# Moving half of the output projection, its addition and its statistics into the last attention pair of a macaron transformer kernel

## The reference, cut to what matters

```python
x = x + 0.5 * ffn(layernorm(x))       # 32 experts, top 8, capacity 128
x = x + attention(layernorm(x))       # 16 heads, causal, ends in "attn @ W_o"
x = x + 0.5 * ffn(layernorm(x))       # the same experts again

def ffn(h):
    logits = h @ gate_weight.T
    topw, topi = top_k(softmax(logits), 8)
    # tokens take their place in each expert's buffer in order (cumulative count of the
    # choices), go through gate/up/silu/down, and are added back by their weight
```

## Time and profile before

| what | us |
|---|---|
| median of 3 runs | 598.95 |
| the 3 runs | 602.34, 598.62, 598.95 |
| the profiled execution | 601.41 |
| its span | 599.4 |

### The profile page before, as it was taken

One profiled execution on the slowest core, in us unless ns is written; L12 is line 12 of the kernel. 1 busy time (PEld: TensorE's weight loads), 2 busy tenths in 40 slices (PEclk: granted clock), 3 DMA queues, 4 the chain that ended last, 5 costly groups with the idle time before them and its releaser, 6 DMA issues.

```text
span 599.4 us, 11028 instructions
## 1 busy us (share of the span) xinstructions
PE 539.6 (90%) x3522; PEld 338.8 (57%) x3546; DVE 425.6 (71%) x1423; ACT 260.3 (43%) x430; POOL 89.8 (15%) x208
## 2 busy tenths in 40 slices
PE   6979999878798999999999999999988876899995
PEld 2856778653454555555555555555533653577774
DVE  5786989764776776767687676767800697689873
ACT  2643212234554555465555546554576241121212
POOL 2320000011601122121212112121222050000000
PEclk8789999987998999999999999999999898899998
DMA  9775100000161000000000000000000440000002
GB/s 190 142 226 177 43 1 3 1 2 2 44 238 55 2 26 29 28 25 11 23 26 26 29 28 25 12 20 28 0 2 1 126 112 1 1 3 2 1 3 70
DMA packets 25094, 26.70 MB, mean 45 GB/s; under 512 B 6704, under 2 KB 18576, under 8 KB 25040
## 3 DMA queue, kind: packets, MB, share of 16 engines
q1 hardware_dynamic: 24176, 25.63, 15.1%
q10 hardware_dynamic: 864, 0.36, 0.2%
HBM read 17.04 MB, written 8.78 MB: 43 GB/s over the span
## 4 chain that ended last, share of the span: by engine, by line
PE 69%; DVE 18%; issue 5%; ACT 4%; DMA 2%; SPq 1%; DVEq 0%; POOL 0%; ACTq 0%
PE ps L1520 12%; PE ps L1585 11%; PE ps L1236 10%; PE ps L1558 9%; PE ps L1320 6%; PE ps L1335 4%; DVE mxh L1078 3%; PE ps L1350 2%; DVE summed L1075 2%; PE ps L1516 2%; DVE xn L802 2%; PE ps L1227 2%; ACT probs L717 2%; PE ps L1162 1%; DMA x<-in_L_attn_x 1%
## 5 line engine op out<-in xcount | busy, mean ns | idle before, releaser
L717 ACT ACTIVATE probs<-ps 128x1024 f32<-128x1024 f32 (+2 forms) x192 | 148.2, 810 | 116.5 <-PE ps L1558 116.4
L1078 DVE TENSOR_REDUCE mxh<-ps 128x1 f32<-128x512 f32 (+2 forms) x176 | 117.4, 690 | 46.3 <-PE ps L1520 44.5
L1520 PE MATMUL ps<-Kst,Qst 120*128 120x512 f32 (+3 forms) x384 | 132.1, 410 | 7.1 <-DVE mxh L1078 3.9
L1520 PEld LDWEIGHTS ps<-Kst,Qst 120*128 120x128 f32 x384 | 66.5, 191 | 64.5 <-DVE mxh L1075 23.3
L1558 PE MATMUL ps<-Qst,Kst 121*128 121x512 f32 (+3 forms) x384 | 95.6, 355 | 1.9 <-ACT probs L717 1.7
L1075 DVE CUSTOM_DVE_ANT_0 summed<-ps,maskf 128x384 f32<-128x384 f32 (+1 forms) x128 | 76.0, 620 | 22.3 <-PE ps L1520 20.3
L490 POOL TENSOR_SCALAR_AFFINE_SELECT probs<-probs 128x256 f32<-128x256 f32 x128 | 52.0, 406 | 220.9 <-ACT probs L717 220.2
L1585 PE MATMUL ps<-probs,Vst 128*32 128x512 f32 (+3 forms) x768 | 81.8, 498 | 1.2 <-POOL probs L490 1.2
L1558 PEld LDWEIGHTS ps<-Qst,Kst 121*128 121x128 f32 x384 | 67.0, 190 | 22.5 <-ACT probs L717 7.3
L1236 PE MATMUL ps<-onehot,xp 128*128 128x512 bf16 (+1 forms) x251 | 68.8, 399 | 9.9 <-DVE onehot L878 8.5
L878 DVE TENSOR_SCALAR onehot<-iotab,posm 128x128 bf16<-128x128 bf16 (+1 forms) x352 | 60.1, 248 | 0.1
(11 more groups left out here) (179 smaller groups left out, 625.1 us busy)
## 6 DMA issues: line engine op xcount, KB each, us to landing
wgn<-in_L_ffn_gate_up_proj SPq DMA_DIRECT2D x8, 384.0 KB, 5.6
guT_d<-gus SPq DMA_DIRECT2D x6, 384.0 KB, 2.8
gus<-guT_d SPq DMA_DIRECT2D x6, 384.0 KB, 6.0
Kst<-kn_d SPq DMA_DIRECT2D x28, 64.0 KB
Qst<-qn_d SPq DMA_DIRECT2D x28, 64.0 KB
wdn<-in_L_ffn_down_proj SPq DMA_DIRECT2D x8, 192.0 KB, 5.9
dnT_d<-dns SPq DMA_DIRECT2D x6, 192.0 KB, 3.9
dns<-dnT_d SPq DMA_DIRECT2D x6, 192.0 KB, 6.9
```

The source lines that it names most:

```text
L717: e.activation(probs[n % RING][:, 2 * b:2 * b + 2, lo:BANK], ps[:, 2 * b:2 * b + 2, lo:BANK], ACT.Exp, scale=SCALE).then_inc(probs_ready, 1)
L1078: e.tensor_reduce(to, s.rearrange("p (q k) -> p q k", k=w), AX.X, ALU.max).then_inc(mx_ready, 1)
L1520: ins = e.matmul(ps[:, bank, i * w:(i + 1) * w], Qst[p][h][0:ROWS, column(b, jt * P):column(b, jt * P) + P], Kst[p][h][0:ROWS, column(b, o ...
```

## The change

For tokens 0 to 511 of both sequences (now called groups 0 and 2, first in the new order HORDER), the last pair of heads is finished by step 8. The change moves these two groups' turning, product with W_o, copy, addition and statistics into the last pair: PE turns them in step 9 and multiplies them in step 10, DVE does the copies, the additions, statistics, mean and variance (`half_early`) ahead of the last `normalise`. After the pair only groups 1 and 3 are left for PE, and DVE begins with the normalised rows of groups 0 and 2; the additions and statistics of groups 1 and 3 come after these, ahead of the first choice of experts (`choose_second`). The stages after attention take the groups in the order 0, 2, 1, 3. The square root's table is loaded ahead of the last copy of attention. The idle products change: 6 and 2 new ones around the last `turn_out`, 2 instead of 20 ahead of the first turned group of rows, and others as shown.

```diff
+HORDER = (0, 2, 1, 3)
+ORDER = ((0, 1, 2, 3), YORDER, HORDER)
+TORDER = ((0, 1, 2, 3), YORDER, HORDER, HORDER)
+WBANK = (6, 7, 2, 3)
...
 (ScalarE)
             pair_step(NPAIR - 1, 1, 0)
+            table_for(ACT.Sqrt)
             copy_values(NPAIR - 1, 1)
-            table_for(ACT.Sqrt)
-            transposed(2)
             root(2, 0)
             root(2, 1)
+            turned_out(2, 2)
+            turned_out(2, 3)
+            first_part(1, 0)
+            first_part(1, 1)
             turned_out(3, 0)
-            root(2, 2)
-            first_part(1, 0)
-            root(2, 3)
             turned_out(3, 1)
             copy_logits(1, 0)
+            root(2, 2)
+            root(2, 3)
             table_for(ACT.Exp)
-            first_part(1, 1)
+            copy_logits(1, 1)
             turned_out(3, 2)
-            copy_logits(1, 1)
             first_part(1, 2)
...
 (VectorE)
+            def half_early():
+                for i in range(RING):
+                    e.wait_ge(turned, 2 * NG + i + 1)
+                    e.tensor_copy(xnT[:, HORDER[i] * BANK:(HORDER[i] + 1) * BANK], ps[:, turn_bank(2, i), :]).then_inc(xnT_ready, 1)
+                for i in range(RING):
+                    add(1, i)
+                for i in range(RING):
+                    stat(2, i)
+                for i in range(RING):
+                    moment(2, i)
+                    variance(2, i)
+                normalise(NPAIR - 1, 1)
+                norm(2, 0)
+
+            def choose_second():
+                norm(2, 1)
+                rest_of(1, 0)
+                add(1, 2)
+                stat(2, 2)
+                add(1, 3)
+                stat(2, 3)
+                moment(2, 2)
+                variance(2, 2)
+                moment(2, 3)
+                variance(2, 3)
+                rest_of(1, 1)
+                norm(2, 2)
+                best(1, 0)
+                norm(2, 3)
+                choice(1, 0)
+                best(1, 1)
+                choice(1, 1)
+                rest_of(1, 2)
+                best(1, 2)
+                choice(1, 2)
+                best(1, 3)
+                choice(1, 3)
...
                 if last:
                     normalise(pair, 0)
+                    half_early()
...
-            normalise(NPAIR - 1, 1)
-            for g in range(NG):
-                add(1, g)
-            front(2)
             route(1)
...
 (TensorE)
+            def project_out(i):
+                g = HORDER[i]
+                e.wait_ge(xnT_ready, 2 * NG + i + 1 + RING)
+                for t in range(g * TG, (g + 1) * TG):
+                    ins = e.matmul(ps[:, WBANK[i], (t - g * TG) * D:(t - g * TG + 1) * D], xnT[:, t * P:(t + 1) * P], wat[:, 4, :], start=True, stop=True)
+                ins.then_inc(wo_done, 1)
...
+                    if last and n == NS - 3:
+                        e.wait_ge(attn_ready, 2 * NPAIR + 1)
+                        for i in range(RING):
+                            turn(2, i, attn)
+                    if last and n == NS - 2:
+                        for i in range(RING):
+                            project_out(i)
                     weighted(n)
...
+            idle_work(0, 6)
             turn_out(NPAIR - 1, 1)
+            idle_work(1, 2)
             e.wait_ge(attn_ready, 2 * NPAIR + 2)
-            transposes(2, attn)
-            for g in range(NG):
-                e.wait_ge(xnT_ready, 2 * NG + g + 1 + RING)
-                e.wait_ge(added, NG + g + 1)
...
-            turn(3, 0, xn, 20)
-            turn(3, 1, xn, 4)
-            logits(1, 0, 2)
+            for i in range(RING, NG):
+                turn(2, i, attn)
+            for i in range(RING, NG):
+                project_out(i)
+            turn(3, 0, xn, 2)
+            turn(3, 1, xn, 2)
+            logits(1, 0, 1)
+            logits(1, 1, 1)
             turn(3, 2, xn, 4)
-            logits(1, 1, 2)
-            turn(3, 3, xn, 4)
+            turn(3, 3, xn, 2)
             logits(1, 2, 2)
             logits(1, 3, 2)
```

More of the change, by code:

```diff
@@ L67, in column, with turn_bank @@
     return (t // BANK * B + b) * BANK + t % BANK
+def turn_bank(n, i):
+    return WBANK[i] if n == 2 and i < RING else i % RING
 def piece(c):
@@ L442, in split @@
                     u = k * NG + g
-                    t = slice(g * TG, (g + 1) * TG)
+                    to = ORDER[2 * k][g]
+                    t = slice(to * TG, (to + 1) * TG)
                     e.wait_ge(rem1, u + 1)
@@ L537, in turned_out @@
             def turned_out(n, i):
-                g = YORDER[i] if n == 1 else i
+                g = TORDER[n][i]
                 e.wait_ge(turned, n * NG + i + 1)
-                e.activation(xnT[:, g * BANK:(g + 1) * BANK], ps[:, i % RING, :], ACT.Copy).then_inc(xnT_ready, 1)
+                e.activation(xnT[:, g * BANK:(g + 1) * BANK], ps[:, turn_bank(n, i), :], ACT.Copy).then_inc(xnT_ready, 1)
             def transposed(n, after=None):
@@ L549, in transposed, with first_part, copy_logits @@
                     after(NG - 1)
-            def first_part(k, g):
+            def first_part(k, i):
+                g = ORDER[2 * k][i]
                 t = slice(g * TG, (g + 1) * TG)
-                e.wait_ge(xn_ready, 2 * k * NT + (g + 1) * TG)
+                e.wait_ge(xn_ready, 2 * k * NT + (i + 1) * TG)
                 e.activation(xp[:, t, 0, :], xn[:, t, :], ACT.Copy).then_inc(part0, 1)
-            def copy_logits(k, g):
-                e.wait_ge(logits_done, k * NG + g + 1)
-                e.activation(flat(lg[:, g * TG:(g + 1) * TG, :]), ps[:, LBANK[k][g % RING], g * TG * E:(g + 1) * TG * E], ACT.Copy).then_inc(lg_copied, 1)
+            def copy_logits(k, i):
+                g = ORDER[2 * k][i]
+                e.wait_ge(logits_done, k * NG + i + 1)
+                e.activation(flat(lg[:, g * TG:(g + 1) * TG, :]), ps[:, LBANK[k][i % RING], g * TG * E:(g + 1) * TG * E], ACT.Copy).then_inc(lg_copied, 1)
             def exps(k):
@@ L764, in add @@
                     e.wait_ge(wo_done, i + 1)
-                    g, bank = i, 2 + i % RING
+                    g, bank = HORDER[i], WBANK[i]
                 else:
@@ L803, in norm, with rest_of, best, choice @@
                                     ALU.subtract, ALU.mult).then_inc(xn_ready, 1)
-            def rest_of(k, g):
-                e.wait_ge(part0, k * NG + g + 1)
-                e.tensor_tensor(rem[g][:, :, :], xn[:, group(g), :], xp[:, group(g), 0, :], ALU.subtract).then_inc(rem1, 1)
+            def rest_of(k, i):
+                g = group(ORDER[2 * k][i])
+                e.wait_ge(part0, k * NG + i + 1)
+                e.tensor_tensor(rem[i][:, :, :], xn[:, g, :], xp[:, g, 0, :], ALU.subtract).then_inc(rem1, 1)
             def wide_of(a, n=E):
                 return a.unsqueeze(2).broadcast_to([P, NT, n])
-            def best(k, g):
-                e.wait_ge(lg_copied, k * NG + g + 1)
+            def best(k, i):
+                g = ORDER[2 * k][i]
+                e.wait_ge(lg_copied, k * NG + i + 1)
                 for t in tiles(g):
                     e.max(t8[:, t, :], lg[:, t, :]).then_inc(top8, 1)
-                e.wait_ge(top8, k * NT + (g + 1) * TG)
+                e.wait_ge(top8, k * NT + (i + 1) * TG)
                 for t in tiles(g):
                     e.match_replace(rep[:, t, :], t8[:, t, :], lg[:, t, :], LOWEST).then_inc(replaced, 1)
[L822 to L826, removed]
+            def choice(k, i):
+                g = group(ORDER[2 * k][i])
+                e.wait_ge(replaced, k * NT + (i + 1) * TG)
+                e.tensor_scalar(maskb[:, g, :], rep[:, g, :], TAKEN, None, ALU.is_lt).then_inc(routed, 1)
+                e.tensor_scalar(rep[:, g, :], rep[:, g, :], TAKEN, UNROUTED, ALU.is_ge, ALU.mult).then_inc(unrouted, 1)
             def pos_of(k, first, last):
@@ L831, in masked_positions @@
             def masked_positions(k, first, last):
-                e.wait_ge(unrouted, k * NG + last)
+                e.wait_ge(unrouted, k * NG + (1 if last == 1 else NG))
                 e.wait_ge(pos_done, 2 * k + 1 + (first > 0))
@@ L892, in more_hots, with choose_first @@
                 hot(c, p, n - 1).then_inc(hot_ready, 1)
-            def route(k):
[L896 to L907, removed]
+            def choose_first():
+                rest_of(0, 0)
+                best(0, 0)
+                norm(0, 3)
+                choice(0, 0)
+                best(0, 1)
+                rest_of(0, 1)
+                choice(0, 1)
+                best(0, 2)
+                rest_of(0, 2)
+                choice(0, 2)
+                best(0, 3)
+                choice(0, 3)
+            def half_early():
[34 more added lines that the diff above has]
+                choice(1, 3)
+            def route(k):
+                if k == 0:
+                    choose_first()
+                else:
+                    choose_second()
                 rest_of(k, 3)
@@ L1154, in turn @@
```

(17 more changed lines are left out.)

7 lines of the change are left out of this document (1 added, 6 removed).

## The result

| | before | after |
|---|---|---|
| median of 7 runs each, us | 598.95 (597.33 to 602.34) | 595.57 (593.47 to 596.69) |
| ratio, with its 95% interval | | 0.9936 [0.9912, 0.9961] |
| profiled execution, us (span) | 601.41 (599.4) | 594.82 (593.0) |

The change makes the kernel 0.64% faster, which is 3.8 us by the ratio; the medians are 3.4 us apart. I forecast 8.4 and a range that ended at 594.4, so the measured time lies outside of it.

What follows compares the result with a forecast made beforehand. Behind the last pair, PE worked while DVE waited, then DVE worked alone; starting DVE at 464.8 instead of 471.59, with 17.85 of work and 0.2 of waits, saves 8.3. Less 0.15 of stalls, 598.95 becomes 590.5 us, range 588.2 to 594.4.

Steps and rivals of the forecast that it cites:

- The change in the pair: Last pair of heads: the moved turns and products cause no wait; the pair ends 1.4 us later, at 462.2.
- Between the pair and VectorE's stretch: From the pair's end to `normalise`: idle products cost 0.55 us on the path; `normalise` ends at 464.8, 1.9 later.
- VectorE's stretch: From `normalise` to the last `choice`: 17.85 us of work plus 0.2 of waits, ending 8.3 earlier.
- the signs that I had named for being wrong: DVE waiting over 1 us, clock 0.5 after 464, a gap in the pair, or another length after the first gather.
- Are its inputs there?: In VectorE's stretch: rows, roots and logits arrive in time, except one short piece behind the last `norm`, adding 0.2 us.
- rival (c): Behind the last pair: the clock falls between 464 and 470, costing 3 us, so 593.5; chance 0.14.
- 4 `norm`: In VectorE's stretch: four normalisations at their old length, 1.32 us each (0.21 for the reciprocal, 1.11 as before).
- The sum: Whole kernel: 8.3 us off the median of 598.95 gives 590.65, and 590.5 with about 0.15 of stalls gone.
- (a): At the first gather: the clock holds there too, gaining 1.2 us more, so 589.3; chance 0.15.
- (b): In VectorE's stretch: ACT's order makes DVE wait some 1.5 us if PE's path is 2 longer: 592.0; chance 0.15.
- (d): From the pair's end to the positions: PE stays at 1.2 GHz and sets the end: 603; chance 0.03.
- (e): The change moves only what something else hides, as the weights' reload; the gain would be 2 us: 597; chance 0.02.

Runs made afterwards that it cites:

- e6_seam3: e3_both with 3 instead of 6 idle products ahead of the last `turn_out`; ratio to the kernel before 0.9858.
- e3_both: The changed kernel with 12 and 8 idle products in TensorE's two pauses and the third group's `norm` ahead of the second `rest_of`; ratio to the kernel before 0.9869.
- e9_late_stats: e3_both with the early groups' additions, statistics, means and variances behind the last `normalise` instead of ahead of it; ratio to the kernel before 0.9959.
- e1_idle: The changed kernel with 12 instead of 4 and 8 instead of 2 idle products ahead of the third and fourth turned groups; ratio to the kernel before 0.9891.
- e2_order: The changed kernel with the third group's `norm` ahead of the second `rest_of` instead of behind it; ratio to the kernel before 0.9898.
- the second profile: The kernel before, unchanged, profiled again; first gather 40.26 us after the start of the last pair's first `normalise`, against 42.67 in the first profile.
- e7_gather_idle: e3_both with 16 idle products between the last positions and the experts; ratio to the kernel before 0.9867.
- e4_before_few: The kernel before with 2 instead of 20 idle products ahead of the first turned group of rows; ratio to the kernel before 1.0035.

## Why the prediction was wrong

**The change in the pair: right.** Forecast: turns and products without a wait, the pair's end 1.4 later. After, the last product with V ends at 460.40, 7.99 from N; before 6.94. So 1.05 later: 16 records took 1.78 on the chain, 2.16 forecast, which is even under the lower bound of 2.0. The square root's table was loaded under TensorE's work (458.50, for 1.28), and no drain stood behind it: the next ACTIVATE started at 459.80.

**Between the pair and VectorE's stretch: right.** `normalise` ends 10.52 from N, 9.06 before: 1.5 later, 1.9 forecast. The three idle products too many cost 0.37 (e6_seam3), forecast 0.55 for all six.

**VectorE's stretch: right in what it holds, wrong in two of its conditions.** Forecast 17.85 of work and 0.2 of waits. With the clock held and the collision away (e3_both) it is 28.25 - 10.52 = 17.7. The terms for the moved additions and statistics were right too: 3.8 computed, 3.7 in e9_late_stats. Two of the signs that I had named for being wrong came in the changed kernel: a wait of 1.5 for logits, and a clock of 0.50 after 464. What failed:
- *"Are its inputs there?"* took all of TensorE's work at 2.4 GHz. Behind `logits(1, 1)` TensorE had four idle products (1.03) and then waited 2.1 for rows, and it was at 1.2 GHz until the last positions. VectorE waited 3.6 instead of 0.2, and e1_idle is 3.3 shorter. This is the mechanism of rival (c), which I put at 464 to 470 and at +3 with a chance of 0.14. I looked for the danger where the kernel before had shown it and where I had counted the idle products that go; it lay in the pause behind them, where the row for "busy 1.03 of 2 and still 1.00" made me sure. That row doesn't carry over: TensorE's pauses there were 0.99 and 0.97 long, and this one 2.09.
- *"4 `norm`"* took them at their old length in a new order. `rest_of(1, 1)` directly ahead of `norm(2, 2)` puts GpSimd's cast and subtraction beside it: +1.27 on its four instructions, 0.9 at the last `choice` (e3_both against e1_idle, e2_order against the changed kernel). I had looked at such meetings only beside the selections in the pair. The chain of the kernel before already held one such `norm`, the fourth group's, 1.43 where the other three took 1.11 or 1.12:

```profile
482.95 1.43 DVE xn L802 x4
```

These two are 4.2 in the traces (e3_both). With both away the traces give 42.67 - 33.64 = 9.0 where the forecast was 8.3: `normalise` came 0.4 earlier than forecast and the stretch was 0.35 shorter.

**The sum: wrong in its base.** I took 8.3 off the median, although it was worked out from one execution that lay 2.5 over the median. I named the 2.5 and did not ask where it was. 2.4 us of difference to the second profile lie in the very stretch that the change rebuilds: the clock of 0.50 from 462 to 468.8, which the second profile doesn't have. Against that profile the changed kernel gains 40.26 - 37.85 = 2.4, against the first 4.8; the runs gave 3.8, in between. In the same way e3_both gains 6.6 or 9.0 in the traces, and about 7.8 in the runs. How often the kernel before has the slow stretch was not measured beyond the three profiles, so how much of the missing gain the base accounts for stays open; the two causes above are seen in the traces whatever the base.

**Rivals.** (a) did not happen in the changed kernel, where the clock was 0.50 in 490 to 492; where it was held (e7_gather_idle) it brought nothing, since the one-hot matrices set the gather's end. (b) did not happen as I had it: VectorE waited 2.3 for logits, but with the order of ScalarE unchanged and the clock held (e1_idle) it waits neither for the roots nor for the logits. e9_late_stats shows that this order can cost a wait, 1.8 for a root. (d) did not happen as a whole: TensorE set the end of the joint in the changed kernel, as (d) has it, but with less than 4 us lost by it and not 12. (e) did not: the DMA share was 0.02 in 482 to 484, and the gather began at 490.

## What to carry to other kernels

A gain read from one profile contains that execution's own accidents: look for stretches at a lower clock inside the part that changes, and count the part from a common point in a second profile before taking the difference off a median. A ratio of many runs and the trace of one of them can also disagree, as in e4_before_few; then the trace does not explain the ratio. When work of TensorE is moved out of a stretch that another engine bounds, what is left is thin: price the rest at 1.2 GHz as well, and fill the pauses with products that nobody reads, up to but not over the wait behind them. A new order on VectorE needs a look at what GpSimd does beside each instruction, not only at the instruction's old duration.

## What the runs showed that I had not expected

One program goes through the same stretch at 1.00 in one execution and at 0.57 in another (461 to 469), 2.4 us apart, and the runs of the kernel before scatter from 595.7 us (mean granted clock 0.971) to 602.9 us (0.957) on one chip. A stretch at 1.2 GHz costs most where it feeds a wait of the engine that sets the end: 3.3 us for the one behind 472, nothing for the one at the first gather, and nothing at the gather for the one in the trace of e4_before_few. Of a group's four 128x128 fp32 normalisations on VectorE, one took 631 ns beside a GpSimd cast of 0.61 us and one 1312 ns beside a subtraction of 1.15 us, while the other two kept their 340; e1_idle has the same, with 1316 ns.
